# Adding the last product of each tile in memory, by an adding DMA from GpSimd's queue, in a fused convolution kernel

## The chip, the cores and the metric

The kernel runs on one core of one Trainium2 chip. The metric is the device time of one execution in microseconds; several executions are timed and their median is given. A profiled execution leaves a trace of every instruction, and all rows below come from one such execution.

## The reference

Input x is 16 images of 256 channels, 56 by 56 pixels, float32. Each image is normalised in 32 groups of 8 channels. The layer works on the normalised image v:

```python
h = depthwise_conv_3x3(v, dw_weight)                 # per channel, padding 1
h = gelu(h)
maps = einsum('bchw,oc->bohw', h, pw_weight) + bias  # 8 * 256 outputs
for i, (dx, dy) in enumerate(OFFSETS8):
    diff = roll(v, shift=(dy, dx), axis=(-2, -1)) - v
    out = out + maps[:, i] * diff
return x + out
```

The kernel folds the term `- v` of all eight directions and the residual x into a ninth map, so that the output of a pixel is the sum of nine maps, each multiplied by a shifted copy of the raw image (the ninth by the unshifted one).

## The kernel before

256 channels are two halves of 128 partitions. An image is cut into 7 tiles of 8 rows, 448 pixels. Two images make a body of 14 tiles (`STEPS`), written out and run in a loop; the last body is written out once more (`loop`, from L197).

For every tile there are nine units (`UNITS`): for each half, four pairs of opposite directions, and a last unit with the ninth map of both halves. The engines share the work of a unit like this:

- TensorE (`make_maps`, up to L668) makes the two maps of a unit in PSUM, six matmuls each: the weights and the hidden tile are each split into a high and a low part. PSUM has room for three units, so a unit waits for VectorE's product of the unit three before it.
- ScalarE (`add_bias`, L449) scales each map and adds its bias in place. Between units it also makes the GELU (L434), the high part of the hidden tile (L439), the normalised rows (L415), the centre tap of the convolution (L427), and the sums and squares of the next image (L349, L358).
- VectorE (`multiply`, L579) multiplies the two maps of a unit by the shifted image. The first pair of a half goes to the accumulator `acc`, the other six to six buffers of `products`, the last unit's to a seventh, `products[:, ADDS]`. Between units it does the other eight taps of the convolution two tiles ahead (L594). In the fourth tile of an image, behind unit 4, it computes the next image's group statistics (`group_stats`, L522 to L547).
- GpSimd, per tile: three additions of products into `acc` (`add_pair`, L284), the low part of the next tile's hidden tile, here called the split (`split_h`, L272), three more additions, and `finish`: the fold (L293), which adds the two members of the pairs into `outb`, and the ninth addition (L297), which adds the ninth product to `outb`. In the fourth tile it also computes the next image's scales (`norm_scales`, L258 to L266) behind the fifth addition.
- SP issues the output DMA of a tile (L232) when the ninth addition is done, and loads the next image when the first tile of an image begins (`load_image`, L207). That load waits until the ninth addition of the tile before is done.

The order on each engine is the order in which the program is written. Semaphores count finished instructions: `prod_s` products, `added_s` additions, `fold_s` folds, `final_s` ninth additions, `out_sent` output DMAs. `acc` and `outb` have two buffers each, taken in turn. VectorE waits for `fold_s` before it writes an `acc` again, and for `final_s` before it writes the one buffer of the ninth product again.

```python
nc.gpsimd.tensor_tensor(o[:], a[:, :, 0, :], a[:, :, 1, :], ALU.add).then_inc(fold_s, 1)

pool.wait_ge(fold_s, n + (1 + FOLD0))
pool.wait_ge(prod_s, n0 * UNITS + ((nl + 1) * UNITS + PROD0))
nc.gpsimd.tensor_tensor(o[:], o[:], products[:, ADDS], ALU.add).then_inc(final_s, 1)
```

At the start GpSimd fills small constants, copies one half of the first image into its padded place in two parts (L253), and later makes the low parts of the weights.

Of the kernel before, what the change touches and what calls it, by code (L numbers as in the profile page):

```python
# [5 lines left out]
def preact_directional_conv(nc, x, pw_t, pw_b, dw, out):  # L6
# [17 lines left out]
    P = 128  # L24
    B, C, H, W = x.shape
# [3 lines left out]
    TILES = H // ROWS  # L29
# [44 lines left out]
    with ctx:  # L74
# [18 lines left out]
        products = sb("products", [P, ADDS + 1, 2, PX])  # L93
# [15 lines left out]
        ones = sb("ones", [P, HALVES])  # L109

# [65 lines left out]
        fold_s = sem("fold_s")  # L176
        final_s = sem("final_s")

        PROD0, ADD0, FOLD0, FINAL0, SENT0 = UNITS, ADDS, 2, 2, 16
# [24 lines left out]
        def _(sp):  # L204
# [18 lines left out]
            def body(n0, b0, last):  # L223
                for nl in range(STEPS):
                    t, par = nl % TILES, (nl // TILES) % 2
                    if t == 0 and not (last and nl):

                        sp.wait_ge(final_s, n0 + (nl + FINAL0))
                        load_image(b0 + par + 1, 1 - par)

                    sp.wait_ge(final_s, n0 + (nl + 1 + FINAL0))
                    sp.dma_start(out_dst[b0 + par, :, :, t * PX:(t + 1) * PX],  # L232
                                 outb[nl % 2][:]).then_inc(out_sent[nl % 2], 16)

            loop(sp, body)
            for par in range(2):
                sp.wait_ge(out_sent[par], 16 * B * TILES // 2 + SENT0)

        @block.gpsimd
        def _(pool):  # L240
# [4 lines left out]
            for par in range(2):  # L245
                nc.gpsimd.memset(xn[par][:], 0.0).then_inc(consts, 1)
            pool.sem_inc(final_s, FINAL0)
            pool.sem_inc(fold_s, FOLD0)
            pool.sem_inc(added_s, ADD0)

# [35 lines left out]
            def finish(n0, nl):  # L286
# [6 lines left out]
                nc.gpsimd.tensor_tensor(o[:], a[:, :, 0, :], a[:, :, 1, :], ALU.add).then_inc(fold_s, 1)  # L293

                pool.wait_ge(fold_s, n + (1 + FOLD0))
                pool.wait_ge(prod_s, n0 * UNITS + ((nl + 1) * UNITS + PROD0))
                nc.gpsimd.tensor_tensor(o[:], o[:], products[:, ADDS], ALU.add).then_inc(final_s, 1)  # L297
# [23 lines left out]
            def body(n0, b0, last):  # L321
                for nl in range(STEPS):
                    t, par = nl % TILES, nl // TILES
                    for i in range(ADDS):
# [3 lines left out]
                        if i == SCALES_AT and t == 3 and not (last and par):  # L328
                            norm_scales(b0 + par + 1, 1 - par)
                    finish(n0, nl)  # L330

# [169 lines left out]
        def _(dve):  # L501
# [47 lines left out]
            def multiply(n0, b, nl, u):  # L549
# [6 lines left out]
                if u == 0:  # L556

                    dve.wait_ge(fold_s, n0 + (nl - 1 + FOLD0))
                if u == LAST:

                    dve.wait_ge(final_s, n0 + (nl + FINAL0))
                    to = products[:, ADDS]
# [140 lines left out]
```

## Time and profile before

| | |
|---|---|
| time, median of 3 runs | 2577.4 us (2575.42 to 2580.82) |
| profiled execution, its own time | 2575.61 us |
| its span in the trace | 2573.8 us |
| mean granted TensorE clock | 0.992 |
| TensorE busy | 2493.1 us (97%) |
| VectorE busy | 2185.1 us (85%) |
| ScalarE busy | 2031.7 us (79%) |
| GpSimd busy | 2182.9 us (85%) |
| HBM read, written | 53.49 MB, 51.38 MB |

The profile names TensorE PE, VectorE DVE, ScalarE ACT, GpSimd POOL and the engine that issues most DMAs SP. A busy share is an average over the program; which engine sets the time is read from the chain of work that ended last, followed back from the last instruction, and from the table of waits. TensorE's matmuls overlap, so its busy time counts them as a stretch without gaps; their pace is read from the length of such a stretch.

### The profile page before, as it was taken

Reading aid. Unit: us, or ns where it says so; the run is one execution under the profiler, and the core shown is the slowest. Engines: PE = TensorE matmul, PEld = TensorE weight load, DVE = VectorE, ACT = ScalarE, POOL = GpSimd, SP = SyncE. Lnnn points to the kernel's source line nnn. Section 1 sums busy time; section 2 is a strip of 40 time slices with the busy share of each in tenths; the row PEclk is TensorE's granted clock in tenths of the full one; section 3 lists DMA queues with packets and bytes.
Section 4 is the critical chain, followed back from the end, with each engine's and each line's share of the span. In section 5 each row is a group of like instructions: output and inputs, shape, how many; then the busy total and the mean of one; then the engine's idle time right before and its main releaser. Section 6 shows DMA issues by size and latency. Waiting matters only on the chain.

```text
span 2573.8 us, 40465 instructions
## 1 busy us (share of the span) xinstructions
PE 2493.1 (97%) x12096; PEld 2284.7 (89%) x12096; DVE 2185.1 (85%) x3033; ACT 2031.7 (79%) x3101; POOL 2182.9 (85%) x1094
## 2 busy tenths in 40 slices
PE   3999999999999999999999999999999999999998
PEld 3899898998989989899898998989898898998997
DVE  7888888888888888888888888888888888888885
ACT  6978878787787877878778797777978878787775
POOL 6898888888889888888888888888798888888888
PEclk9999999999999999999999999999999999999999
DMA  4003020030300303012030210303003030030000
GB/s 129 27 23 72 23 66 22 23 72 22 74 15 22 72 22 73 23 41 53 16 73 22 63 31 23 73 16 72 22 23 74 22 72 15 22 72 22 22 22 22
DMA packets 46042, 107.95 MB, mean 42 GB/s; under 512 B 2896, under 2 KB 31568, under 8 KB 45520
## 3 DMA queue, kind: packets, MB, share of 16 engines
q1 hardware_dynamic: 45776, 104.88, 15.1%
q8 instruction: 108, 1.77, 0.3%
q14 instruction: 158, 1.29, 0.2%
HBM read 53.49 MB, written 51.38 MB: 41 GB/s over the span
## 4 chain that ended last, share of the span: by engine, by line
PE 88%; DVE 5%; ACT 4%; issue 3%; POOL 0%; DMA 0%; ACTq 0%; DVEq 0%; POOLq 0%; SPq 0%
PE psum L668 88%; DVE psum L594 2%; ACT psum L449 2%; DVE products L579 1%; ACT squares_out L358 1%; DVE moments L523 1%; ACT hid L434 1%; ACT hhi L439 0%; DMA products<-x 0%; ACT psum L427 0%; DVE acc L579 0%; POOL acc L284 0%; DVE mom_t L527 0%; DVE dev_t L533 0%; DVE dev_t L535 0%
## 5 line engine op out<-in xcount | busy, mean ns | idle before, releaser
L449 ACT ACTIVATE psum<-psum,bias,rstd 128x448 f32<-128x448 f32 x2016 | 1354.0, 696 | 513.6 <-PE psum L668 508.1
L284 POOL TENSOR_TENSOR acc<-acc,products 128x896 f32<-128x896 f32 x672 | 1429.8, 2128 | 338.5 <-DVE products L579 314.6
L668 PE MATMUL psum<-hhi,w_hi 128*128 128x448 f32 x4032 | 1487.7, 369 | 71.4 <-ACT hhi L439 38.4
L668 PE MATMUL psum<-hhi,w_lo 128*128 128x448 f32 x4032 | 1484.1, 368 | 0.0
L594 DVE SCALAR_TENSOR_TENSOR psum<-xn,dw_f,psum 128x448 f32<-128x448 f32 x1792 | 1137.8, 680 | 68.9 <-ACT psum L427 68.8
L668 PE MATMUL psum<-hlo,w_hi 128*128 128x448 f32 x4032 | 1155.6, 368 | 0.3 <-POOL hlo L272 0.3
L579 DVE TENSOR_TENSOR products<-psum,xpad 128x896 f32<-128x896 f32 x784 | 852.7, 1088 | 246.0 <-ACT psum L449 212.8
L668 PEld LDWEIGHTS psum<-hhi,w_hi 128*128 128x128 f32 x4032 | 762.7, 189 | 147.4 <-ACT hhi L439 38.4
L668 PEld LDWEIGHTS psum<-hlo,w_hi 128*128 128x128 f32 x4032 | 762.0, 189 | 67.0 <-POOL hlo L272 0.9
L668 PEld LDWEIGHTS psum<-hhi,w_lo 128*128 128x128 f32 x4032 | 763.0, 189 | 65.4
L579 DVE TENSOR_TENSOR acc<-psum,xpad 128x896 f32<-128x896 f32 x224 | 243.1, 1085 | 51.3 <-ACT psum L449 50.4
L297 POOL TENSOR_TENSOR outb<-outb,products 128x896 f32<-128x896 f32 x112 | 238.0, 2125 | 16.6 <-POOL outb L293 14.6
L293 POOL TENSOR_TENSOR outb<-acc 128x896 f32<-128x896 f32 x112 | 238.0, 2125 | 12.8 <-POOL acc L284 7.8
L272 POOL TENSOR_TENSOR hlo<-hid,hhi 128x896 fp32r<-128x896 f32 x112 | 238.5, 2130 | 2.4 <-ACT hhi L439 2.4
L415 ACT ACTIVATE xn<-xpad,shift,rstd 128x560 f32<-128x560 f32 (+1 forms) x224 | 190.1, 849 | 4.5 <-POOL bias L266 4.5
L427 ACT ACTIVATE psum<-xn,dw_f 128x448 f32<-128x448 f32 x224 | 134.3, 631 | 4.5
L434 ACT ACTIVATE hid<-psum 128x896 f32<-128x896 f32 x112 | 102.1, 912 | 6.2 <-DVE psum L594 6.2
L439 ACT CAST hhi<-hid 128x896 fp32r<-128x896 f32 x112 | 104.6, 934 | 0.0
L358 ACT ACTIVATE squares_out<-xpad,neg_mean_c 128x1568 f32<-128x1568 f32 x60 | 96.3, 1606 | 0.0
L349 ACT ACTIVATE squares_out<-xpad 128x1568 f32<-128x1568 f32 x60 | 91.6, 1526 | 0.0
L258 POOL TENSOR_TENSOR rstd<-var_eps,neg_half 128x2 f32<-128x2 f32 x16 | 13.1, 821 | 11.1 <-DVE neg_mean L547 11.1
L523 DVE TENSOR_SCALAR moments<-neg_mean_c 128x2 f32<-128x2 f32 x16 | 16.0, 1000 | 0.0
(56 smaller groups left out, 166.8 us busy)
## 6 DMA issues: line engine op xcount, KB each, us to landing
out<-outb SPq DMA_DIRECT2D x112, 448.0 KB, 2.5
xpad<-x SPq DMA_DIRECT2D x30, 1568.0 KB, 15.3
products<-x SPq DMA_DIRECT2D x4, 784.0 KB, 6.9
xpad<-pw_t SPq DMA_DIRECT2D x1, 2048.0 KB, 12.2
dw_f<-dw SPq DMA_DIRECT2D x1, 9.0 KB, 8.0
pb_f<-pw_b SPq DMA_DIRECT2D x1, 8.0 KB, 8.1
```

The lines of the kernel that those rows point to most:

```text
L272: nc.gpsimd.tensor_tensor(hlo[par][:], hid[par][:], hhi[par][:].bitcast(F32), ALU.subtract).then_inc(hlo_s, 1)
L284: nc.gpsimd.tensor_tensor(a, a, products[:, i], ALU.add).then_inc(added_s, 1)
L293: nc.gpsimd.tensor_tensor(o[:], a[:, :, 0, :], a[:, :, 1, :], ALU.add).then_inc(fold_s, 1)
L297: nc.gpsimd.tensor_tensor(o[:], o[:], products[:, ADDS], ALU.add).then_inc(final_s, 1)
L358: nc.scalar.activation(squares_out[:], rows, ACT.Square, bias=neg_mean_c[:, g:g + 1], accum_out=part_sq[:, g, c:c + 1]).then_inc(measure, 1)
L415: nc.scalar.activation(xn[par][:, g, r0:r1, 1:W + 1], xpad[ip][:, g, t * ROWS + r0:t * ROWS + r1, 1:W + 1], ACT.Identity, bias=shift[ip][: ...
L427: nc.scalar.activation(conv[:, g, :].rearrange("p (r c) -> p r c", c=W), xn[par][:, g, 1:1 + ROWS, 1:1 + W], ACT.Copy, scale=dw_f[:, g, CE ...
L434: nc.scalar.activation(hid[nl % 2][:], conv, ACT.Gelu).then_inc(gelu_s, 1)
L449: nc.scalar.activation(m, m, ACT.Identity, bias=bias[ip][:, g, d:d + 1], scale=rstd[ip][:, g:g + 1]).then_inc(biased_s, 1)
L579: nc.vector.tensor_tensor(to.rearrange("p s (r c) -> p s r c", c=W), maps(q).rearrange("p s (r c) -> p s r c", c=W), window(xpad_t[ip][:, ...
L594: nc.vector.scalar_tensor_tensor(d, xn[nl % 2][:, g, ky:ky + ROWS, kx:kx + W], dw_f[:, g, TAPS_DVE[j]:TAPS_DVE[j] + 1], d, ALU.mult, ALU.a ...
L668: last = nc.tensor.matmul(maps(q)[:, side, :], w[:, kk, col:col + P], h[par][:, kk, :], start=s == 0, stop=s == len(steps) - 1)
```

## The change

The ninth addition is taken out of `finish`; the fold is then the instruction that completes `outb`, and it raises `final_s`. SP sends `outb` to memory as before, now without the ninth product. A new `add_ninth` issues a DMA on GpSimd's queue that adds the ninth product to the same place of the output in memory. It waits for the tile's output DMA and for the ninth product. In the program it stands one tile later, behind the fifth addition, and once more at the end of each body for its last tile. The ninth product gets a second buffer, and VectorE waits before it writes one for the adding DMA of two tiles before. The semaphores of these DMAs get their first value from two small DMAs of one column at the start. SP's image load waits for the products of the tile before in place of its ninth addition. At the end SP waits for the adding DMAs too.

```diff
--- before.py
+++ after.py
@@ -90,7 +90,7 @@
         hlo = [sb(f"hlo{i}", [P, HALVES, PX], F32R) for i in range(2)]
         acc = [sb(f"acc{i}", [P, HALVES, 2, PX]) for i in range(2)]
 
-        products = sb("products", [P, ADDS + 1, 2, PX])
+        products = sb("products", [P, ADDS + 2, 2, PX])
 
         assert (ADDS + 1) * 2 * PX >= HALVES * H * W
         first = products[:].rearrange("p a s x -> p (a s x)")[:, 0:HALVES * H * W]
@@ -107,6 +107,7 @@
         zeros = sb("zeros", [P, HALVES, 1, WP])
         neg_half = sb("neg_half", [P, HALVES])
         ones = sb("ones", [P, HALVES])
+        spare = [sb(f"spare{i}", [P, 1]) for i in range(2)]
 
         squares_out = sb("squares_out", [P, SROWS, W])
         part_sums = sb("part_sums", [P, HALVES, SLICES])
@@ -173,10 +174,10 @@
         biased_s = sem("biased_s")
         prod_s = sem("prod_s")
         added_s = sem("added_s")
-        fold_s = sem("fold_s")
         final_s = sem("final_s")
-
-        PROD0, ADD0, FOLD0, FINAL0, SENT0 = UNITS, ADDS, 2, 2, 16
+        ninth_sent = [sem(f"ninth_sent{i}") for i in range(2)]
+
+        PROD0, ADD0, FINAL0, SENT0 = UNITS, ADDS, 2, 16
         MEASURES = 2 * HALVES * SLICES + HALVES
         STAT = 14
         SCALES = 4
@@ -225,7 +226,8 @@
                     t, par = nl % TILES, (nl // TILES) % 2
                     if t == 0 and not (last and nl):
 
-                        sp.wait_ge(final_s, n0 + (nl + FINAL0))
+
+                        sp.wait_ge(prod_s, n0 * UNITS + (nl * UNITS + PROD0))
                         load_image(b0 + par + 1, 1 - par)
 
                     sp.wait_ge(final_s, n0 + (nl + 1 + FINAL0))
@@ -235,6 +237,7 @@
             loop(sp, body)
             for par in range(2):
                 sp.wait_ge(out_sent[par], 16 * B * TILES // 2 + SENT0)
+                sp.wait_ge(ninth_sent[par], 16 * B * TILES // 2 + SENT0)
 
         @block.gpsimd
         def _(pool):
@@ -244,9 +247,12 @@
             nc.gpsimd.memset(moments[:], 0.0).then_inc(consts, 1)
             for par in range(2):
                 nc.gpsimd.memset(xn[par][:], 0.0).then_inc(consts, 1)
+            pool.wait_ge(consts, CONSTS)
             pool.sem_inc(final_s, FINAL0)
-            pool.sem_inc(fold_s, FOLD0)
             pool.sem_inc(added_s, ADD0)
+
+            for i in range(2):
+                pool.dma_start(spare[i][:], zeros[:, 0, 0, 0:1]).then_inc(ninth_sent[i], SENT0)
 
             for c in range(SLICES):
                 pool.wait_ge(first_in[0][c], 16)
@@ -290,11 +296,16 @@
                 pool.wait_ge(added_s, n0 * ADDS + ((nl + 1) * ADDS + ADD0))
 
                 pool.wait_ge(out_sent[nl % 2], n0 * 8 + (16 * (nl // 2) + SENT0))
-                nc.gpsimd.tensor_tensor(o[:], a[:, :, 0, :], a[:, :, 1, :], ALU.add).then_inc(fold_s, 1)
-
-                pool.wait_ge(fold_s, n + (1 + FOLD0))
+                nc.gpsimd.tensor_tensor(o[:], a[:, :, 0, :], a[:, :, 1, :], ALU.add).then_inc(final_s, 1)
+
+            def add_ninth(n0, b0, nl):
+
+
+                i, t, par = nl % 2, nl % TILES, (nl // TILES) % 2
+                pool.wait_ge(out_sent[i], n0 * 8 + (16 * (nl // 2 + 1) + SENT0))
                 pool.wait_ge(prod_s, n0 * UNITS + ((nl + 1) * UNITS + PROD0))
-                nc.gpsimd.tensor_tensor(o[:], o[:], products[:, ADDS], ALU.add).then_inc(final_s, 1)
+                pool.dma_start(out_dst[b0 + par, :, :, t * PX:(t + 1) * PX], products[:, ADDS + i],
+                               accum_op=ALU.add).then_inc(ninth_sent[i], 16)
 
 
             pool.wait_ge(consts, CONSTS)
@@ -327,7 +338,10 @@
                         add_pair(n0, nl, i // (NP - 1), i % (NP - 1) + 1)
                         if i == SCALES_AT and t == 3 and not (last and par):
                             norm_scales(b0 + par + 1, 1 - par)
+                        if i == ADDS - 2 and nl:
+                            add_ninth(n0, b0, nl - 1)
                     finish(n0, nl)
+                add_ninth(n0, b0, STEPS - 1)
 
             loop(pool, body)
 
@@ -555,11 +569,12 @@
                     dve.wait_ge(wraps, b * 4 + 4)
                 if u == 0:
 
-                    dve.wait_ge(fold_s, n0 + (nl - 1 + FOLD0))
+                    dve.wait_ge(final_s, n0 + (nl - 1 + FINAL0))
                 if u == LAST:
 
-                    dve.wait_ge(final_s, n0 + (nl + FINAL0))
-                    to = products[:, ADDS]
+
+                    dve.wait_ge(ninth_sent[nl % 2], n0 * 8 + (16 * (nl // 2) + SENT0))
+                    to = products[:, ADDS + nl % 2]
                 elif k == 0:
                     to = acc[nl % 2][:, g]
                 else:
```

On GpSimd, at the end of an ordinary tile (the third of a body): the last two of the six additions, the fold, the ninth addition and the first addition of the next tile, before:

```order
L284 TENSOR_TENSOR acc<-acc,products 128x896
L278 REGISTER_ALU
L282 REGISTER_ALU
L284 TENSOR_TENSOR acc<-acc,products 128x896
L290 REGISTER_ALU
L292 REGISTER_ALU
L293 TENSOR_TENSOR outb<-acc 128x896
L295 REGISTER_ALU
L296 REGISTER_ALU
L297 TENSOR_TENSOR outb<-outb,products 128x896
L278 REGISTER_ALU
L284 TENSOR_TENSOR acc<-acc,products 128x896
```

and the same place now:

```order
L290 TENSOR_TENSOR acc<-acc,products 128x896
L306 REGISTER_ALU
L307 ISA
L307 DMA out<-products 128x2x448
L284 REGISTER_ALU
L288 REGISTER_ALU
L290 TENSOR_TENSOR acc<-acc,products 128x896
L296 REGISTER_ALU
L299 TENSOR_TENSOR outb<-acc 128x896
L284 REGISTER_ALU
L290 TENSOR_TENSOR acc<-acc,products 128x896
```

The addition behind the fold is gone, and the DMA (of the tile before) stands between the fifth and the sixth addition.

On GpSimd, the last two tiles of the program, before:

```order
L284 TENSOR_TENSOR acc<-acc,products 128x896 x3
L293 TENSOR_TENSOR outb<-acc 128x896
L297 TENSOR_TENSOR outb<-outb,products 128x896
L284 TENSOR_TENSOR acc<-acc,products 128x896 x6
L293 TENSOR_TENSOR outb<-acc 128x896
L297 TENSOR_TENSOR outb<-outb,products 128x896
```

and now:

```order
L307 DMA out<-products 128x2x448
L290 TENSOR_TENSOR acc<-acc,products 128x896
L299 TENSOR_TENSOR outb<-acc 128x896
L290 TENSOR_TENSOR acc<-acc,products 128x896 x5
L307 DMA out<-products 128x2x448
L290 TENSOR_TENSOR acc<-acc,products 128x896
L299 TENSOR_TENSOR outb<-acc 128x896
L307 DMA out<-products 128x2x448
```

Two DMAs fall into the last tile: that of the tile before it and its own, which is the program's last work.

On GpSimd at the start, now (before, the row of the DMAs is not there):

```order
L247 MEMSET moments 128x32
L249 MEMSET xn 128x1160 x2
L255 DMA spare<-zeros 128x1 x2
L259 COPY xpad<-products 128x28x56 x2
```

The two small DMAs stand ahead of the copies of the first image.

## Rows read from the trace of the kernel before

**Rows 1.** The page: busy shares, and the chain that ended last by engine
```profile
PE 2493.1 (97%) x12096; PEld 2284.7 (89%) x12096; DVE 2185.1 (85%) x3033; ACT 2031.7 (79%) x3101; POOL 2182.9 (85%) x1094
...
PE 88%; DVE 5%; ACT 4%; issue 3%; POOL 0%; DMA 0%; ACTq 0%; DVEq 0%; POOLq 0%; SPq 0%
```
**Rows 2.** The chain's longest pieces over the span: start us, length us, what
```profile
40.63 71.45 PE psum L668 x344
...
761.71 138.91 PE psum L668 x684
...
1705.19 143.14 PE psum L668 x684
```
**Rows 3.** Who waited for whom: us in total, times, longest us
```profile
POOL acc L284 <- DVE products L579: 314.6, 329, 3.7
...
PE psum L668 <- DVE products L579: 31.5, 15, 2.3
DVE products L579 <- POOL acc L284: 28.1, 54, 0.6
```
**Rows 4.** The chain from 60 to 260 us: start us, length us, what
```profile
59.97 52.12 PE psum L668 x257
...
124.31 0.98 DVE moments L523
...
128.76 131.33 PE psum L668 x639
```
**Rows 5.** Busy time by stretch; the last three numbers: granted clock, DMA share, GB/s
```profile
130.90:135.00 4.10, 4.10 (x18) 3.75 (x17) 4.10 (x6) 2.09 (x3) 3.80 (x6) 0.80 0.00 0
...
1780.00:1800.00 20.00, 20.00 (x98) 18.16 (x97) 17.08 (x23) 15.03 (x23) 16.90 (x9) 1.00 0.84 179
```
**Rows 6.** GpSimd's timeline in an ordinary tile: start us, length us, what, idle before
```profile
176.38 2.12 POOL L284 TENSOR_TENSOR acc<-acc,products 128x896 f32<-128x896 f32 x1 [0.29 <-DVE products L579]
178.59 2.13 POOL L293 TENSOR_TENSOR outb<-acc 128x896 f32<-128x896 f32 x1
180.87 2.12 POOL L297 TENSOR_TENSOR outb<-outb,products 128x896 f32<-128x896 f32 x1 [0.16 <-POOL outb L293]
183.60 2.12 POOL L284 TENSOR_TENSOR acc<-acc,products 128x896 f32<-128x896 f32 x1 [0.61 <-DVE products L579]
```
**Rows 7.** Output DMA's issue (ns) and landing (us); image load, us to landing
```profile
L232 SPq DMA_DIRECT2D out<-outb x112: 372/372/418, 69.9 to 2570.8; - x112
...
DMA to landing us min/median/max: 2.5/2.5/4.4
...
xpad<-x SPq DMA_DIRECT2D x30, 1568.0 KB, 15.3
```
**Rows 8.** Timelines of GpSimd and of ScalarE at the start
```profile
5.62 1.50 POOL L253 COPY xpad<-products 128x1568 f32<-128x1568 f32 x1 [2.56 <-DMA products<-x]
...
17.04 0.37 ACT L341 COPY xpad<-xpad 128x112 f32<-128x112 f32 x1
```
**Rows 9.** VectorE's second statistics instruction: duration ns min/median/max
```profile
L523 DVE TENSOR_SCALAR moments<-neg_mean_c x16: 158/1056/1078, 17.3 to 2333.0; 128x2 f32<-128x2 f32 x16
```
**Rows 10.** GpSimd's timeline in the fourth tile of two images
```profile
121.04 2.14 POOL L284 TENSOR_TENSOR acc<-acc,products 128x896 f32<-128x896 f32 x1 [1.05 <-DVE products L579]
123.13 2.13 POOL L272 TENSOR_TENSOR hlo<-hid,hhi 128x896 fp32r<-128x896 f32 x1
...
437.53 2.13 POOL L284 TENSOR_TENSOR acc<-acc,products 128x896 f32<-128x896 f32 x1 [1.49 <-DVE products L579]
```
**Rows 11.** Timelines of GpSimd and of SP at the end
```profile
2561.93 2.12 POOL L284 TENSOR_TENSOR acc<-acc,products 128x896 f32<-128x896 f32 x1 [0.36 <-DVE products L579]
2564.41 2.07 POOL L284 TENSOR_TENSOR acc<-acc,products 128x896 f32<-128x896 f32 x1 [0.36 <-DVE products L579]
2566.56 2.08 POOL L293 TENSOR_TENSOR outb<-acc 128x896 f32<-128x896 f32 x1
2568.72 2.07 POOL L297 TENSOR_TENSOR outb<-outb,products 128x896 f32<-128x896 f32 x1
...
2570.81 0.37 SPq L232 DMA_DIRECT2D out<-outb  x1
```

## The prediction

> **What bounds the kernel now.** I read the page's busy shares and chain first, then TensorE's stretches, then who waits for whom, then GpSimd's timeline in one ordinary tile, in the tile that computes the statistics, and at the two ends of the program.
>
> TensorE is busy 97% of the span, and 88% of the chain that ended last is its one matmul line; GpSimd has 0% of that chain [rows 1]. Its work is regular: a stretch of 684 matmuls takes 138.91 to 143.14 us [rows 2], 203 to 209 ns each, so a unit of 12 takes 2.44 to 2.51 us and a tile of nine units about 22 us; 12096 matmuls at 203 ns are 2456 of the 2573.8 us. The rest is the start (TensorE first works at 40.63 us [rows 2]), about 12 us at the end, and one break in each of 15 images. TensorE's waits say the same: 31.5 us in 15 waits for VectorE's products [rows 3], and none of any size for GpSimd. The 15 breaks are the fourth tile of an image, where VectorE computes the statistics: the chain leaves TensorE at 112.08 and comes back at 128.76, through ScalarE's and VectorE's lines alone [rows 4]. Behind the break the granted clock reads 0.80 over 4.1 us [rows 5], that is partly at the 1.2 GHz level, after TensorE had stood idle; so a break costs more than its wait.
>
> GpSimd is busy 85% [rows 1], and it mostly waits itself: 314.6 us in 329 waits for VectorE's products [rows 3]. An ordinary tile is seen in [rows 6]: the sixth addition, the fold and the ninth addition start 2.2 to 2.3 us apart, each takes 2.12 or 2.13 us, and even after the ninth addition GpSimd waits 0.61 us for VectorE before it can begin the next tile. VectorE waits for GpSimd only 28.1 us in 54 waits of at most 0.6 us [rows 3], and none of these is in the chain. GpSimd is a follower, not a limit.
>
> **The change, part by part.** *Removed:* 112 ninth additions of 2.12 us [rows 6], 237 us of GpSimd's time. *Added:* 112 DMA issues on GpSimd's queue, each of which also waits for the tile's plain output DMA; two small DMAs at the start; one more product buffer.
>
> In the middle the removed 2.1 us per tile are worth **nothing**. They lie beside TensorE's work, and the instruction behind them waits for VectorE anyway [rows 6]. What the issue costs there is hidden as long as GpSimd keeps up. Its eight instructions that stay start 2.2 us apart at the closest [rows 6], 17.6 us, of a tile of 21.9 us; so an issue may take 4.3 us before GpSimd sets the pace. No row shows a DMA issued by GpSimd. The nearest are SP's issue of the same bytes, 0.37 us [rows 7], GpSimd's copy, 1.50 us [rows 8], and GpSimd's addition, 2.12 us [rows 6]. I take 1.5 us, the one-input instruction of this engine, with 0.37 and 2.12 as ends. All three are under 4.3.
>
> The waits in the middle are also free. GpSimd issues tile n's adding DMA behind the fifth addition of tile n+1, some 17 us after tile n's output DMA was issued, which lands in 2.5 us, 4.4 at most [rows 7]. VectorE waits for it only before the last product of tile n+2: more than 20 us later. SP issues each output DMA 2.2 us earlier and the image load with it, and neither was waited for in the loop. The DMA engines are at their busiest while an image is loaded, a share of 0.84 over 20 us of the 157 us of an image [rows 5]. The adding DMA must read the output, read the product and write: three passes instead of two. It doubles the traffic of the output or a little more, and there is room. VectorE's and ScalarE's instructions in the loop are unchanged but for that wait.
>
> In the fourth tile the new DMA stands behind the small scale instructions and not ahead of them, so the next image's bias isn't later. One thing there does depend on GpSimd: VectorE's second statistics instruction takes 1056 ns in the median and 158 ns at the least [rows 9]. In this break it stands in the chain until 125.29 [rows 4], and GpSimd's split, begun at 123.13, ends at 125.26 [rows 10]; it looks held until the split is done. I leave that hold as it is (its own case stands below).
>
> At the **start** the two small DMAs stand behind the memsets and ahead of the copies, which begin at 5.62 after 2.56 us of waiting [rows 8]. Two issues of 2.12 us would move them by 1.7 us. The copied half is first wanted at 17.04, by ScalarE [rows 8]: nothing.
>
> At the **end** nothing hides anything; this is the sum. Before [rows 11]: fifth addition until 2564.05, sixth 2564.41 to 2566.48, fold 2566.56 to 2568.64, ninth addition 2568.72 to 2570.79, SP's issue at 2570.81, landing 2.5 us later at 2573.3, end 0.5 us behind.
> - The adding DMA of the last tile but one now stands between the fifth and sixth additions. Issued at 2564.14 for 1.5 us, the sixth starts at 2565.72 in place of 2564.41: 1.3 us later. The fold ends at 2569.95.
> - The output DMA is issued at 2570.04 and lands at 2572.5; that is 0.8 us before now, what is left of the saved addition.
> - The last adding DMA can begin only then: 0.1 us to wake, 1.5 us of issue, then the transfer. The plain DMA takes 2.5 us, its issue of 0.37 included [rows 7]. For three passes, a read of HBM that must come back before the write among them, I take twice the 2.5, less the 0.37 of issue, 4.6 us. It ends at 2578.7, and the program 0.5 us later at 2579.2.
>
> **Sum: +5.4 us** on the profiled span of 2573.8. The ends: issue 0.37 and landing 2.5 give about +0.7 us; issue 2.12 and a landing like the 15.3 us of half an image's load [rows 7] give +17 us. The profiled execution took 2575.61 us, 1.8 us under the median of 2577.4; added to the median I get 2582.8 us.
> The Trainium skill, DMA: Bandwidth & Descriptors, "Anatomy of one DMA", gives about 2.0 us plus the bytes over 436 GB/s for a DMA issued by GpSimd: an estimate of 3.1 us for these 448 KB. By it the end would be near 2576.2 with the same delays, +2.4 us, but it doesn't speak of adding. No row here shows either.
>
> **The rivals.**
> - *Cheap tail, not slower.* One place, the two dependent DMAs behind the last fold: if GpSimd's issue and the landing together are under about 5.9 us rather than the 6.1 I take, the total is within 0.2%. At 4 us it is 2580.7, at the low ends 2578.1. For it: 2.5 us is what the plain DMA of these bytes takes, and the engines are idle then. Against: the extra pass, and that GpSimd's issue is surely no cheaper than SP's.
> - *Faster, through the held statistics instruction.* If the relieved GpSimd ran its split earlier in the fourth tile, VectorE's 0.9 us hold would go in 15 images: 13.5 us on the breaks that the chain runs through, less the tail: 2582.8 − 13.5 = 2569.3 us, and more if the clock then stays up. The Trainium skill, SBUF — State Buffer, "Who interferes with whom", has the mechanism: a VectorE instruction in a two-port mode and a GpSimd instruction shut each other out of a shared pair of ports. The trace agrees that one ends with the other. Against the case: in both breaks shown GpSimd waits 1.05 and 1.49 us for VectorE ahead of the third addition [rows 10], with the split right behind it, so a GpSimd with less to do runs its split no earlier.
> - *GpSimd becomes the bound.* From an issue of 4.3 us on; at 6 us, 1.7 × 112 = 190 us, 2773 us. VectorE's wait for the adding DMA would show it too. For it: the cost appears in no row. Against: it is twice what one of this engine's additions takes, and nothing of the 448 KB passes through the engine itself.
> - *The pace moves by itself.* TensorE's stretches of 684 differ by 4.2 us with no wait in them [rows 2], and the three runs differ by 5.4 us. If other stretches fall on the slow pace, some us either way come on top of any case.
>
> **How the numbers follow.** This measurement tells about 0.2%, 5.2 us, from no change. The sum gives +5.4, right at that line. Tail dearer than 5.2 us: 0.44; cheap tail: 0.42; GpSimd bound or a late DMA that VectorE waits for: 0.05; faster hold or pace: 0.09, of which 0.07 beyond 0.2%. So faster 0.07, same 0.44, slower 0.49. The predicted time is the sum's, 2582.8. For 8 in 10: down to 2576.5 (the low ends with a pace 1.6 us better), up to 2591 (a landing of about 12 us; the 15.3 us stand for 3.5 times the bytes).
>
> **What would show it.** After: GpSimd busy about 240 us less but for the issues, its waits for VectorE longer by what is saved; TensorE's 31.5 us in 15 waits and the statistics instruction at 1056 ns unchanged; the last two DMAs one behind the other in the last 9 us. Wrong would be: a GpSimd issue over 4 us, waits of VectorE for a DMA, a changed number of TensorE waits, or an end within 2 us of the old one.

## The result, and the profile after

The changed kernel takes 2599.77 us in the median of 7 runs (2590.02 to 2610.01); the kernel before, timed beside it, 2575.42 us (2567.53 to 2582.0). The ratio is 1.0099, 95% interval 1.0069 to 1.0128: **about 1% slower, some 25 us**, five times the loss that was forecast and outside the range. The profiled span went from 2573.8 to 2597.0 us, 23.2 us, so the profile holds the loss. Of all executions below one is left out of its ratio: the kernel with a single unrelated load once took 3505.25 us at a granted clock of 0.658.

The page of the changed kernel: span, busy shares, the DMA queues, and the two groups on GpSimd that changed. The columns are those of [rows 1]; in the groups, busy us and mean ns, then idle time before them and its releaser.

```profile
span 2597.0 us, 40763 instructions
...
PE 2495.4 (96%) x12096; PEld 2285.1 (88%) x12096; DVE 2185.4 (84%) x3033; ACT 2034.3 (78%) x3101; POOL 2081.7 (80%) x1096
...
q1 hardware_dynamic: 45776, 104.88, 14.8%
q0 software_dynamic: 30528, 51.39, 14.4%
...
L290 POOL TENSOR_TENSOR acc<-acc,products 128x896 f32<-128x896 f32 x672 | 1477.7, 2199 | 441.3 <-DVE products L594 389.7
...
L307 POOL DMA_DIRECT2D out<-products x112 | 134.6, 1202 | 39.1 <-DMA out<-outb 29.5
...
out<-outb SPq DMA_DIRECT2D x112, 448.0 KB, 2.5
out<-products POOLq DMA_DIRECT2D x112, 448.0 KB, 5.6
```

GpSimd is busy 101 us less (2182.9 before, [rows 1]) and waits for VectorE's products 75 us more (314.6 before, [rows 3]). An adding DMA costs it 1.20 us of issue and lands 5.6 us behind the start of the issue, where SP's plain DMA of the same bytes takes 2.5. The new queue moves half the bytes of the other and takes nearly the same share of the DMA engines, 14.4% against 14.8%.

Who waited for whom in the changed kernel, as in [rows 3]:

```profile
PE psum L683 <- DVE products L594: 31.0, 15, 2.4
...
POOL out L307 <- DMA out<-outb: 29.5, 8, 3.9
...
PE psum L683 <- DVE acc L594: 15.0, 6, 2.7
```

The 15 breaks for the statistics stand as they were (31.0 against 31.5 us). New are six waits of TensorE for the first product of a tile, 15.0 us, and eight waits of GpSimd for an output DMA, 29.5 us. The loop over bodies runs seven times and so goes back to its start six times; a body ends eight times. The six waits are at the loop's back edge. One of them, by engine: ScalarE's last maps of the old body and the first of the new one, VectorE's, GpSimd's and SP's work around it (timelines; start us, length us).

```profile
676.84 0.70 ACT L463 ACTIVATE psum<-psum,bias,rstd 128x448 f32<-128x448 f32 x1 [0.52 <-PE psum L683]
680.08 2.55 ACT L463 ACTIVATE psum<-psum,bias,rstd 128x448 f32<-128x448 f32 x4 [2.54 <-PE psum L683]
...
685.83 1.09 DVE L594 TENSOR_TENSOR acc<-psum,xpad 128x896 f32<-128x896 f32 x1 [5.98 <-ACT psum L463]
...
676.02 1.20 POOL L307 DMA_DIRECT2D out<-products  x1
...
685.42 1.19 POOL L307 DMA_DIRECT2D out<-products  x1 [3.85 <-DMA out<-outb]
693.67 6.53 POOL L290 TENSOR_TENSOR acc<-acc,products 128x896 f32<-128x896 f32 x3 [7.06 <-DVE products L594]
...
681.73 0.37 SPq L234 DMA_DIRECT2D out<-outb  x1
682.74 9.86 SPq L208 DMA_DIRECT2D xpad<-x  x2
```

Every engine has its own branch back to the start of the loop, and the trace has a row for it: the branch (`COMPARE_BRANCH`) and the first thing that the engine does at the loop's top (`FUSED_REGOPS`). These are the rows of the loop's line at this edge, start us at the end, in the changed kernel:

```profile
L200 ACTq COMPARE_BRANCH  x1: 45/45/45, 676.9 to 676.9; - x1
...
L200 DVEq COMPARE_BRANCH  x1: 63/63/63, 677.9 to 677.9; - x1
L200 ACTq FUSED_REGOPS  x1: 59/59/59, 680.0 to 680.0; - x1
...
L200 DVEq FUSED_REGOPS  x1: 74/74/74, 682.9 to 682.9; - x1
...
L200 POOLq COMPARE_BRANCH  x1: 53/53/53, 685.5 to 685.5; - x1
L200 POOLq FUSED_REGOPS  x1: 64/64/64, 693.5 to 693.5; - x1
```

and VectorE's at the same edge in the kernel before:

```profile
L199 DVEq COMPARE_BRANCH  x1: 62/62/62, 674.9 to 674.9; - x1
...
L199 DVEq FUSED_REGOPS  x1: 74/74/74, 677.7 to 677.7; - x1
```

Two things are to be seen. First, the way back costs every engine something in the kernel before too: over its six edges 2.5 to 2.8 us on ScalarE, 2.8 to 3.1 on VectorE, 2.6 to 2.8 on GpSimd, without a semaphore to wait for. In the changed kernel ScalarE's is hardly longer (3.1 us here, 2.5 to 3.4 over the six), but VectorE's is 5.1 us here and 4.7 to 5.1 over the six. ScalarE has finished the first two maps of the new body at about 681.4; VectorE multiplies them only at 685.83, and TensorE runs out of free PSUM. (The row of VectorE's product names ScalarE as what ended the wait. That is inferred from semaphores, and the maps that this product needs were long done.) Second, GpSimd waits 3.85 us for the output DMA at the body's end, issues the last DMA of the body, and needs 8.0 us from its branch back to the loop's top; its first addition of the new body starts at 693.67. The image load was issued at 682.74. In the kernel before, that addition follows the ninth one by 2.3 us.

What the DMA engines do meanwhile can be asked for stretch by stretch. The profile has queues of their own for instructions. Between 677.9 and 681.1 us, first line, no packet of theirs begins, and the adding DMA has the engines; between 681.1 and 683, second line, two do, and VectorE goes on at 682.94:

```profile
q0 software_dynamic: 256, 0.44, 91.8%
...
q14 instruction: 2, 0.02, 2.1%
```

The end, from the timelines, and two of SP's own waits: for the last adding DMA, and the program's very last wait (L74):

```profile
2583.91 2.07 POOL L299 TENSOR_TENSOR outb<-acc 128x896 f32<-128x896 f32 x1
2588.82 1.20 POOL L307 DMA_DIRECT2D out<-products  x1 [2.83 <-DMA out<-outb]
...
SPq L240 <- DMA out<-products: 5.9, 1, 5.9
SPq L74 <- PEq L74: 2.2, 1, 2.2
```

VectorE's last product ends at 2583.26 and the span 13.7 us later; before it was 6.6 us (2567.18 to 2573.8). So 7.1 us are lost at the end and 15.0 us in the six waits, together 22.1 of 23.2. That the sum comes out so near is in part luck: TensorE's time without its waits, summed from its matmul rows, also moved, by +7.3 us over the six bodies between the first and the last (1867.5 to 1874.8 us) and by -5.9 us in the last body (312.9 to 307.0 us). The granted clock has a part in it (0.83 over 682 to 692 us, behind the wait). The question for the experiments was what causes the waits at the back edge.

### The profile page after: what moved, and what is told of

It reads as the page before. It is cut to its first block, busy times and chain, and to the rows that moved or that the text cites. A ratio compares the mean times of both kernels' runs of the same rounds, so it can differ in the third digit from the quotient of the medians.

```text
span 2597.0 us, 40763 instructions
## 1 busy us (share of the span) xinstructions
PE 2495.4 (96%) x12096; PEld 2285.1 (88%) x12096; DVE 2185.4 (84%) x3033; ACT 2034.3 (78%) x3101; POOL 2081.7 (80%) x1096
## 3 DMA queue, kind: packets, MB, share of 16 engines
q1 hardware_dynamic: 45776, 104.88, 14.8%
q0 software_dynamic: 30528, 51.39, 14.4%
HBM read 53.49 MB, written 102.76 MB: 60 GB/s over the span
## 4 chain that ended last, share of the span: by engine, by line
PE 85%; ACT 5%; DVE 4%; issue 4%; POOL 1%; DMA 0%; ACTq 0%; DVEq 0%; POOLq 0%; SPq 0%
PE psum L683 85%; ACT psum L463 2%; DVE psum L609 2%; DVE products L594 1%; ACT squares_out L372 1%; ACT hid L448 1%; ACT psum L441 0%; DVE moments L537 0%; ACT hhi L453 0%; DMA products<-x 0%; ACT xn L429 0%; DVE acc L594 0%; POOL hlo L278 0%; POOL acc L290 0%; POOL rstd L264 0%
## 5 line engine op out<-in xcount | busy, mean ns | idle before, releaser
L290 POOL TENSOR_TENSOR acc<-acc,products 128x896 f32<-128x896 f32 x672 | 1477.7, 2199 | 441.3 <-DVE products L594 389.7
L307 POOL DMA_DIRECT2D out<-products x112 | 134.6, 1202 | 39.1 <-DMA out<-outb 29.5
```

Of the source, the lines that this page charges most:

```text
L290: nc.gpsimd.tensor_tensor(a, a, products[:, i], ALU.add).then_inc(added_s, 1)
L307: pool.dma_start(out_dst[b0 + par, :, :, t * PX:(t + 1) * PX], products[:, ADDS + i], accum_op=ALU.add).then_inc(ninth_sent[i], 16)
```

## The experiments

Each ratio is to the kernel before, timed beside it on the same chip. Of the longer edits the diffs show the part that matters.

**Shortening the DMA in flight at the back edge.** The adding DMA of the last tile but one of each body moves 16 of 128 partitions; the other 112 partitions of that tile lack their ninth product.

```diff
+                ps = 16 if nl == STEPS - 2 else P
-                pool.dma_start(out_dst[b0 + par, :, :, t * PX:(t + 1) * PX], products[:, ADDS + i],
+                pool.dma_start(out_dst[b0 + par, 0:ps, :, t * PX:(t + 1) * PX], products[0:ps, ADDS + i],
```

> The adding DMA of the thirteenth tile of each body, which is issued in the body's last tile just as the engines go back to the loop's start, moves 16 of the 128 partitions only (7/8 of that tile's ninth product is left out of the output). Theory A: that transfer delays the instruction fetch behind the loop's back edge; the six waits of TensorE for VectorE's acc (15.0 us) disappear, at least four of six, each back-edge tile falls back to within 1 us of an ordinary one, and the total is 12 to 20 us under the changed kernel's 2600, about 2583. Rival B: it is GpSimd's own late return into the loop (its wait for the output DMA at the body's end, 3.85 us) that holds the others: the six waits stay, time within 4 us of the changed kernel. Rival C: the earlier image load at the back edge: the six waits stay too.

Measured: 2593.16 us, ratio 1.0089 (1.0062 to 1.0116). Not the 12 to 20 us that theory A wanted. But the six waits did go, VectorE's way back is 2.8 to 2.9 us again, and other waits came. GpSimd's and TensorE's:

```profile
POOL acc L290 <- issue: 45.9, 6, 8.1
...
PE psum L684 <- POOL hlo L278: 12.8, 7, 2.3
```

Now TensorE waits 12.8 us for GpSimd's split (`hlo`), one tile later. Theory A alone falls; it names one of two things.

**Shortening the body's last DMA instead** (the same edit with `STEPS - 1`).

> The same shortening, but of the adding DMA of the fourteenth tile, which GpSimd issues at the body's end behind the wait for the output DMA (7/8 of that tile's ninth product is left out). Theory A: the fetch is over by then, so the six waits of TensorE for acc stay and the loop costs what it does in the changed kernel; only the program's last DMA is shorter, so the total is 0 to 4 us under the changed kernel's 2600. Rival C, traffic beside the image load: the six waits go or shrink.

Measured: 2595.84 us, ratio 1.0102 (1.0051 to 1.0152). The six waits for `acc` stay, 15.4 us; SP's last wait for the adding DMA falls from 5.9 to 2.7 us. The bytes of the body's last DMA are not the cause.

**Issuing the DMA earlier, nothing left out.**

```diff
-                        if i == ADDS - 2 and nl:
+                        if i == (1 if nl == STEPS - 1 else ADDS - 2) and nl:
```

> Nothing left out: in the body's last tile alone the adding DMA is issued behind the second addition instead of the fifth, some 9 us earlier, so that it has landed when the engines go back to the loop's start. Theory A: as in the shortened one, the six waits for acc go and the total is 12 to 20 us under the changed kernel, about 2583. Rival B (GpSimd late at the body's end): nothing changes there, 2600 within 4 us.

Measured: 2594.16 us, ratio 1.0098 (1.0068 to 1.0127), the same picture as the first: no waits for `acc`, but

```profile
POOL acc L290 <- issue: 46.7, 6, 8.0
...
PE psum L683 <- POOL hlo L278: 13.0, 7, 2.4
```

**An unrelated load at the same place in the kernel before.**

```diff
+                        if i == ADDS - 2 and nl == STEPS - 1:
+                            pool.wait_ge(extra_s, b0 * 8 + 16)
+                            pool.dma_start(unused[:], x_src2[b0]).then_inc(extra_s, 16)
```

> The kernel before, with an unrelated load of the same 448 KB issued by GpSimd behind the fifth addition of each body's last tile (and one at the start), into a tile that nobody reads. Nothing of the change is in it. Theory A: any transfer at this place delays the fetch: ScalarE's gap at the back edge grows from 2.0 us and TensorE waits there; as this load takes some 3 us in place of 5.6, at least two of the six edges show it and the kernel is 3 to 18 us slower than before. Theory A in its narrow form (only adding traffic does it) and rivals B and C: the edges stay as before, within 3 us of the kernel before.

Measured: 2573.87 us, ratio 1.0004 (0.9980 to 1.0028): no difference in time, where 3 to 18 us were expected. The profile has six waits for `acc` of 3.6 us in all. The mechanism does show in it: ScalarE's way back takes 4.0 to 4.2 us at all six edges in place of 2.5 to 2.8, and VectorE's 3.2 to 3.8 in place of 2.8 to 3.1. TensorE has enough in hand to hide nearly all of that.

From here the theory (A2 in the expectations) was: there are two causes, and either makes TensorE wait once per edge. One is the transfer under way while ScalarE and VectorE go back; the other is GpSimd's own late return behind its wait for the output DMA. When TensorE has already been held by the first, the second is hidden behind it.

**Each cause by itself.** For the last tile of each body the ninth product is added by GpSimd as before, so nothing is waited for at the body's end; the early issue is the edit above.

```diff
+                if nl == STEPS - 1:
+                    nc.gpsimd.tensor_tensor(o[:], a[:, :, 0, :], a[:, :, 1, :], ALU.add).then_inc(fold_s, 2)
+                    pool.wait_ge(fold_s, b0 + 2)
+                    pool.wait_ge(prod_s, n0 * UNITS + ((nl + 1) * UNITS + PROD0))
+                    nc.gpsimd.tensor_tensor(o[:], o[:], products[:, ADDS + nl % 2], ALU.add).then_inc(final_s, 1)
+                    return
```

> The changed kernel, but the last tile of every body (8 of 112) gets its ninth product by GpSimd's addition, so that no wait for the output DMA and no DMA stands at the body's end and at the program's end; the adding DMA of the tile before it stays behind the fifth addition. Theory A2 (two causes at the back edge, either of which makes TensorE wait once: the transfer that delays the others' fetch, and GpSimd's own late return behind its wait for the output DMA): the six waits of TensorE for acc stay (first cause), GpSimd's 7 to 8 us gap behind the edge shrinks to 2 to 4 us, and the total falls by the tail alone, 5 to 9 us, to about 2592. Rival B2 (all is GpSimd's late return): the edge tiles fall to within 1 us of ordinary ones and the time to about 2575.

> Both cures together: the body's last tile by GpSimd's addition, and the adding DMA of the tile before it behind the second addition. 104 of 112 ninth products still go by the adding DMA. Theory A2: neither the waits for acc at the back edge nor the waits for the split one tile later (7 waits, 13.0 us with the early issue alone) are left, the tail is as before; the time is within 4 us of the kernel before, about 2574. If the adding DMAs cost something in the ordinary tiles too, it stays 8 us or more above the kernel before.

Measured: the addition alone, 2588.10 us, ratio 1.0071 (1.0046 to 1.0096). With the early issue too, 2574.77 us, ratio 1.0018 (0.9998 to 1.0037): **the loss is gone, with 104 of 112 ninth products still added by DMA**. With the addition alone GpSimd's gap is 3.28 us and TensorE's six waits for `acc` remain at 10.0 us. It is VectorE that comes back late, as in the changed kernel (4.7 to 5.1 us); this time the table of waits shows it without a releaser:

```profile
DVE acc L600 <- issue: 31.7, 6, 5.4
...
PE psum L689 <- DVE acc L600: 10.0, 6, 1.8
```

With both edits TensorE's waits for `acc` are one of 0.3 us, and the wait for the split is the first tile's 0.3 us. The upper end of the interval bounds what the ordinary adding DMAs can cost: 0.37%, or 9.5 us for 104 of them.

**GpSimd's wait alone, in the kernel before.**

```diff
                     finish(n0, nl)
+                pool.wait_ge(out_sent[1], n0 * 8 + (16 * TILES + SENT0))
```

> The kernel before, with one wait added: at each body's end GpSimd waits until the tile's output DMA has landed, and then goes back to the loop's start. No DMA of GpSimd at all. Theory A2: GpSimd's return, 2.6 us later, falls beside the image load, its gap behind the edge grows from 2.3 to 6 us or more, and one tile later TensorE waits for the split in some of six edges: 5 to 18 us slower than before. Rival (the wait is harmless, it is the DMA issue that makes GpSimd late): the gap grows by the 2.6 us alone and the time stays within 3 us of the kernel before.

Measured: 2597.48 us, ratio 1.0115 (1.0081 to 1.0150). **One wait of some 2.5 us at the end of each of the eight bodies costs as much as the whole change**, and more than the 5 to 18 us expected. GpSimd's timeline around the edge, SP's, and the waits:

```profile
679.48 2.12 POOL L297 TENSOR_TENSOR outb<-outb,products 128x896 f32<-128x896 f32 x1 [0.16 <-POOL outb L293]
693.76 6.48 POOL L284 TENSOR_TENSOR acc<-acc,products 128x896 f32<-128x896 f32 x3 [12.17 <-issue]
...
682.76 9.19 SPq L207 DMA_DIRECT2D xpad<-x  x2
...
PE psum L669 <- POOL hlo L272: 22.6, 7, 4.1
```

The output DMA issued at 681.76 lands at about 684.6; GpSimd branches at 684.71 and is at the loop's top 8.9 us later, at 693.61. Over 682 to 694 us the DMA engines are 0.89 busy. From 684.5 to 691.5 us, first line below, the image load alone has them and no packet of an instruction queue begins; two do between 691.5 and 693.7, the other lines:

```profile
q1 hardware_dynamic: 394, 1.41, 96.9%
...
q8 instruction: 1, 0.02, 3.9%
q14 instruction: 1, 0.01, 1.7%
```

The split follows three additions later and TensorE waits for it.

**The same wait, with the image load held back.**

```diff
+                        if nl == 0:
+                            sp.wait_ge(prod_s, n0 * UNITS + (4 + PROD0))
                         load_image(b0 + par + 1, 1 - par)
-            MEASURE_AT = ((1, 0), (1, 3), ...
+            MEASURE_AT = ((1, 2), (1, 3), ...
```

> The kernel before with the same wait at each body's end that made it 1.15% slower (27 us), and the load of the body's second image held back until the fourth product of the body's first tile, some 9 us; the first of the next image's sums is moved two units back so that it doesn't wait for the load. Theory A3 (GpSimd's return is slow because its instruction fetch runs beside the image load): its gap behind the edge falls from 12.2 us to 4 to 6 us, TensorE's seven waits for the split (22.6 us) go, and the time is within 6 us of the kernel before. Rival (the return is slow because GpSimd is the last engine to go back, load or not): gap and waits stay, over 20 us slower than before.

Measured: 2574.48 us, ratio 1.0005 (0.9985 to 1.0024). The wait is still there and no cost is seen:

```profile
684.59 0.37 SPq L234 DMA_DIRECT2D out<-outb  x1
691.21 9.22 SPq L207 DMA_DIRECT2D xpad<-x  x2
...
690.27 6.54 POOL L286 TENSOR_TENSOR acc<-acc,products 128x896 f32<-128x896 f32 x3 [5.84 <-issue]
...
PE psum L671 <- POOL hlo L274: 0.3, 1, 0.3
```

GpSimd's first addition starts 3.2 us after the landing (684.59 + 2.5 to 690.27), and its way back takes 2.5 to 2.7 us at the six edges in place of 8.0 to 9.3. What made the late return slow was the image load beside it.

**Two unrelated loads in the kernel before**, the edit of the single one doubled.

> The kernel before, with two unrelated loads of 448 KB each issued by GpSimd behind the fifth addition of each body's last tile, so that the transfers last about as long as the one adding DMA does. One such load made the six edge tiles 6.1 us long in excess in place of 2.8, without a difference in the times. Theory A2, first cause (a transfer in flight delays the fetch of the engines that go back): TensorE's waits for VectorE's acc at the six edges sum to 8 us or more, the excess of the six edge tiles to 10 to 20 us, the time 4 to 18 us over the kernel before. Rival (only adding traffic does it): excess under 7 us, time within 4 us of before.

Measured: 2586.42 us, ratio 1.0057 (1.0038 to 1.0077); TensorE's waits for `acc` 8.9 us in 6, before them VectorE has gaps of up to 5.1 us with nothing shown that it waits for:

```profile
DVE acc L594 <- issue: 19.8, 4, 5.1
...
PE psum L683 <- DVE acc L594: 8.9, 6, 1.7
```

So a plain transfer does it as well, if it lasts long enough; that it adds is not needed. Both causes are now made in the kernel before, without the change. Engine by engine it is plainer still. From the branch to the loop's top (start to start of the two rows of the loop's line), us, least and most of the six edges:

| kernel | ScalarE | VectorE | GpSimd |
|---|---|---|---|
| before | 2.5 to 2.8 | 2.8 to 3.1 | 2.6 to 2.8 |
| changed | 2.5 to 3.4 | 4.7 to 5.1 | 8.0 to 8.6 |
| changed, adding DMA issued early | 2.5 to 2.9 | 2.8 to 3.1 | 8.6 to 9.0 |
| changed, last tile by addition | 2.5 to 3.0 | 4.7 to 5.1 | 2.5 to 2.8 |
| both of these | 2.6 to 2.9 | 2.8 to 2.9 | 2.5 to 2.8 |
| before, GpSimd's wait | 2.5 to 2.9 | 2.8 to 3.0 | 8.0 to 9.3 |
| the same, image load held back | 2.6 to 2.9 | 2.8 to 3.0 | 2.5 to 2.7 |
| before, two unrelated loads | 3.9 to 4.4 | 4.2 to 4.6 | 2.6 to 2.8 |

Each cure takes away the delay of one engine and leaves the other's.

**The tail alone.** In the changed kernel the program's very last tile is added by GpSimd.

> The changed kernel, but the program's very last tile gets its ninth product by GpSimd's addition as before; all other 111 keep the adding DMA. The tail in the changed profile is 13.7 us from the end of VectorE's last product to the end of the span, 6.6 before. Theory T (the tail is two DMAs in a row, issue, landing of 5.6 us and a drain behind): the tail falls back to 6.5 to 9 us and the time by 5 to 7 us, to about 2593; the six waits at the loop's back edge stay. Rival: the end of a program that has used GpSimd's DMA queue costs its 2.5 us whatever comes last: the tail stays at 9 us or more.

Measured: 2593.51 us, ratio 1.0104 (1.0076 to 1.0132). The interval is 7 us either way, so the times don't tell; the profile does. The tail is 8.3 us, in the forecast 6.5 to 9. SP's last waits:

```profile
SPq L240 <- DMA out<-outb: 2.1, 1, 2.1
SPq L74 <- PEq L74: 0.5, 1, 0.5
```

The 5.9 us for the adding DMA are gone (what is waited for is the output DMA, 2.1), and the last wait falls from 2.2 to 0.5 us. It is 2.1 or 2.2 us in all four kernels that end with a DMA of GpSimd, the one with the shortened last DMA among them, and 0.2 us in all others but this one.

**The held statistics instruction.** In the fourth tile the split goes ahead of the third addition, in the kernel before and in the repaired form of the change.

```diff
-                        if i == SPLIT_H_AT and not (last and nl + 1 >= STEPS):
+                        if i == (2 if t == 3 else SPLIT_H_AT) and not (last and nl + 1 >= STEPS):
```

> The kernel before; in each fourth tile alone GpSimd's split stands ahead of the third addition instead of behind it. Nothing of the change is in it. The rival of the prediction said that the split holds VectorE's second statistics instruction. Theory H (held by the running GpSimd instruction until that ends): its median falls from 1056 ns to under 400 ns in most of the 15 breaks, the breaks shorten by 0.5 to 0.9 us each and the time falls by 5 to 18 us, to about 2562. Rival: the instruction takes its microsecond in the loop whatever GpSimd does (1056 ns stays, time within 3 us of before).

> The repaired form of the change (last tile of a body by addition, adding DMA of the tile before it behind the second addition; 2574.8 against 2570.1) with the split ahead of the third addition in the fourth tile. If theory H holds it falls by 5 to 18 us as well, to about 2564, and is then equal to the kernel before with the same edit within 5 us; it should not be faster than that one, since GpSimd's relief is worth nothing.

Measured: on the kernel before 2539.83 us, ratio 0.9868 (0.9841 to 0.9896); on the repaired change 2535.57 us, ratio 0.9859 (0.9833 to 0.9886). **Both beat the two kernels of this study by over 30 us**, and their intervals overlap: a cost of the adding DMAs is not seen here either. The fall itself is well over the 5 to 18 us expected of it. In the kernel before with the edit:

```profile
L523 DVE TENSOR_SCALAR moments<-neg_mean_c x16: 158/161/165, 17.4 to 2311.4; 128x2 f32<-128x2 f32 x16
...
120.01 2.12 POOL L272 TENSOR_TENSOR hlo<-hid,hhi 128x896 fp32r<-128x896 f32 x1
122.10 2.13 POOL L284 TENSOR_TENSOR acc<-acc,products 128x896 f32<-128x896 f32 x1
...
PE psum L668 <- DVE products L579: 18.0, 15, 1.4
...
130.90:135.00 4.10, 4.10 (x22) 3.80 (x21) 4.10 (x7) 2.53 (x4) 3.94 (x6) 1.00 0.02 4
```

GpSimd uses the time in which it waited for VectorE (120.01 in place of [rows 10]'s 121.04), is done at 124.23, and the statistics instruction at 124.26 takes 0.16 us; its median falls from 1056 ns [rows 9] to 161. The 15 breaks cost 18.0 us in place of 31.5. That is 13.5 us of the 32.4 between the medians (2572.18 to 2539.83). The clock has part of the rest: over 130.9 to 135 us it reads 1.00 instead of 0.80 [rows 5], and 0.999 over the program instead of 0.992. TensorE stood idle a shorter time before it and did not fall toward the 1.2 GHz level. The profiled span fell by 23.9 us, less than the medians, and how the remainder divides between the clock and TensorE's own pace was not settled.

## Why the prediction was wrong

**The ordinary tiles: right.** The removed addition was worth nothing, the issue (1.20 us, taken as 1.5) is hidden, GpSimd's waits for VectorE grew, the 15 breaks and the statistics instruction (1054 ns after) did not change. The repaired form is the test: 1.0018 with 104 of the adding DMAs in it.

**The step that failed** is the sentence "The waits in the middle are also free", and with it "there is room" for the traffic. That the adding DMA stands "behind the fifth addition of tile n+1, some 17 us after" the output DMA is true of 104 of the 112 tiles only. I weighed each wait by who needs the data, and the traffic by the DMA engines' mean share. Neither looked at the one place where the middle is not regular, the loop's back edge. There every engine needs 2.5 us and more from its branch to the loop's top, and nobody's data are late, so no wait for data shows it. The change put two things at that place. A transfer issued 1.9 us before VectorE's branch in the edge above and running through the 3.2 us behind it, which made VectorE's way back 5 us in place of 3; and, because the last adding DMA of a body isn't carried into the next tile, GpSimd's wait for the output DMA in front of its own branch, so that its way back falls beside the image load and takes 8 us. The diff showed both: `add_ninth(n0, b0, STEPS - 1)` stands behind the loop over tiles, inside the body. What is priced at 0 in my sum measured 15.0 us of waiting in the six edges. The prediction named a changed number of TensorE's waits as a sign of being wrong, and that is the sign that came.

**The tail: right in kind, too small.** Forecast +5.4 us, in the profile +7.1. The last fold ends 2.7 us behind VectorE's last product in place of 1.5, so the issue ahead of it delays it by the 1.3 us that were forecast. SP waits 5.9 us for the adding DMA behind the output DMA's landing; the sum had 6.2 for the wake, the issue and the transfer. (That its transfer is three passes over memory was not shown: the page's count of bytes written to HBM doubles, and that of bytes read stays.) What was missed is the program's last wait, 2.2 us against 0.2 before.

**The rivals.** "GpSimd becomes the bound" was priced by the length of the issue in every tile; its issue is far under the 4.3 us. The late return of GpSimd at six back edges is another mechanism and was not among them. "Faster, through the held statistics instruction" was rightly not expected of this change, since the split follows an addition that waits for VectorE; but its mechanism is real, and its price was put at 13.5 us where moving the split gave over 30.

**The pace** moved by some us either way from body to body, as the rival had it, and in these two profiles it nearly cancels (+7.3 and -5.9 us). It does not explain the loss: the kernel with both cures and the one with the load held back are within 0.4% of the kernel before.

## What to carry to other kernels

Look at a loop's back edge as a stage of its own: ask what each engine does in the last microseconds before its branch, and what transfers are under way when it branches. A wait for a DMA at the end of a loop body delays the engine's way back into whatever transfer comes next; with that transfer held back, the same wait cost nothing that could be measured here. Issue such work a few steps earlier, or do it another way in the body's last step. The table of waits shows the first engine that runs dry and infers its releaser; the rows of the loop's own line tell which engine was late. When a fix removes one wait and the time stays, read the table of waits again before dropping the theory: here a second cause stood right behind the first.

## What the runs showed of the hardware that was not expected

- From its branch to the loop's top an engine took 2.5 to 3.1 us here with little DMA traffic beside it. Beside one adding DMA VectorE took 4.7 to 5.1 us, beside two plain loads ScalarE 3.9 to 4.4 and VectorE 4.2 to 4.6, beside an image load GpSimd 8.0 to 9.3 us (in the last, the DMA engines were 0.89 busy). Twice the stretch was looked at packet by packet: no packet of the instruction queues began for 3.2 us and for 7.0 us, while one data transfer had the engines, and the late engine went on within 2.1 us of the next ones. The profile doesn't say which engine such a packet is for, so that the fetch is what holds the engine is inferred, from this and from the trials.
- An adding DMA of 448 KB from SBUF to HBM lands 5.6 us after its issue begins, SP's plain one in 2.5. Not all of that is the adding: a plain load of 448 KB that GpSimd issued landed in 4.5 us (3.9 to 4.8). The page counts the adding DMA's bytes as written once, and HBM's reads did not grow (53.49 MB). Its issue holds GpSimd 1.20 us.
- When the last work of a program is a DMA of GpSimd, the program's last wait is 2.1 to 2.2 us, against 0.2 to 0.5 us.
- VectorE's small statistics instruction waits until a running split of GpSimd ends, 0.9 us here. With that hold gone the granted clock behind the break shown reads 1.00 in place of 0.80, and 0.999 over the program.
